# Selective-scan kernel: one quad of states from dt*u scaled by ScalarE and turned by TensorE, other units for the diagonals, both halves' softplus in one place

## The chip, the cores and the metric

One Trainium2 chip, one NeuronCore. The metric is the device time of one execution of the whole program in microseconds (us), lower is better. The engines are TensorE (PE; its weight loads are listed as PEld), VectorE (DVE), ScalarE (ACT), GpSimd (POOL) and SyncE (SP), which issues most DMAs.

## What is computed

A block of a vision model on x of 8 x 64 x 64 x 96, float32: group norm, a two-dimensional selective scan (192 channels, 16 states, 4 directions over 4096 places), a residual, and a second layer with a spectral up- and downsampling. The change lies in the scan alone:

```python
xs = ...                                   # (8, 4 directions, 192, 4096)
x_dbl = einsum('bkdl,kcd->bkcl', xs, x_proj_w)
dts, Bs, Cs = x_dbl[:, :, :6], x_dbl[:, :, 6:22], x_dbl[:, :, 22:]
delta = softplus(einsum('bkrl,kdr->bkdl', dts, dt_proj_w) + dt_proj_b)
A = -exp(A_logs)
def step(h, inp):                          # over the 4096 places
    ul, dl, Bl, Cl = inp
    h = exp(dl[..., None] * A) * h + (dl * ul)[..., None] * Bl[:, :, None, :]
    return h, einsum('bkdn,bkn->bkd', h, Cl)
y = ys + xs * Dk
```

## The kernel before

The program has three phases, one after the other: the first makes the scan's input xa and the gate, the second (`scan_phase`, from L309) does the scan, the third sums the directions and does everything behind. The change is in the second.

**Chunks, steps, units.** The scan is cut into 128 chunks: 8 images x 4 directions x 4 pieces of TC = 1024 places, in the order of `KORDER`. A chunk has two steps, one for each half of 96 channels; `un` counts units, 12 in a step (numbers 0 to 11 are the even step, 12 to 23 the odd one). A unit is 128 rows (4 states x 32 channels) x 1024 places: the 16 states are four groups g of four ("quads"), the 96 channels three thirds j = x % 3. `ORDER` = (2, 2, 2, 0, 3, 3, 3, 0, 1, 1, 1, 0) names the group of each of the 12 units.

**One unit**: ACT makes the decay E = exp(A * delta) (L841) from `dlr`, delta repeated by DMA. PE writes the drive dt*u*B into a PSUM bank ("fill"). DVE scans (L761) into H. POOL multiplies H by C (L961, "weigh") into HC. PE sums HC over the states (L700, `sum_y`, six matmuls for each half of the columns of three units).

**Three sorts of fill.** Group 0 is DIRECT: PE spreads B by `selb` (L642) and DVE multiplies it by `dur`, dt*u repeated by DMA (L742). The other three are DIAGONAL: PE multiplies the turned dt*u (`dluT`, weights of 32 columns) by diagonal matrices that hold B, 32 matmuls for a unit (L677; each float32 matmul is two records). The diagonals of groups 3 and 1 are made by ACT (L831, 64 multiplications of 128 x 128 in a chunk, `DIAGS` says how many after which unit), those of group 2 by POOL (L950, two in a chunk, after the weighing of units 17 and 19: `POOL_AT` = (6, 8) in the odd step).

**Side jobs in the row of PE.** `x` projects u for the next chunk (L627), `dt` makes the input of softplus (L636), `lt` turns dt*u of a step (L657; before an even step also B, L652). ACT copies the projection (L795, L796), DVE splits it (L736), ACT does softplus (L807) with a table load before it and another before the next exp, POOL makes dt*u (L942), ACT copies the turned block (L820). Units and side jobs take the three PSUM banks (`NP`) of `ring` in turn: each must wait until what stood in its bank three places earlier is released (a unit by its scan, `x` by DVE's split, `dt` by softplus, `lt` by ACT's copy).

**Other waits that order the work.** H has 4 buffers, so DVE scans unit un only after POOL weighed un - 4. E has 3. HC has 6, so POOL weighs un only after the sum over the group that ended at un - 4 or before (`y_summed`). The sum for the first group of a step also adds, in a second direction, what an earlier direction stored (L690), and for direction 0 a skip term (L696). `dlr` has 5 slots (`NSLOT`), `dur` 3 (`NDUR`); SP issues their loads in the order that `sync` writes out, and waits in it. The lines that set the row of side jobs:

```python
            if x == 1:
                jobs += [("lt", n + 1)]
            if x == 4 and c < NCHUNK:
                jobs += [("x", c)]
```

## Time and profile before

| | us |
|---|---|
| median of 3 runs (lowest, highest) | 11437.5 (11436.28, 11439.11) |
| the profiled execution: time, span | 11433.25, 11431.5 |
| PE busy, matmuls | 10219.9 (89%) |
| DVE busy | 9414.9 (82%) |
| ACT busy | 8518.6 (75%) |
| POOL busy | 9042.7 (79%) |
| mean granted clock of TensorE | 0.960 |

The span is from the first to the last instruction; the execution's own time is 1.75 us more. The first scan starts at 648.84 us and the scan phase ends near 9800 us, so it takes four fifths of the time. Matmuls are pipelined and their ends are modelled, so a busy PE isn't PE at its peak. A row of the waits says which engine and line waited, whose instruction ended the wait, how long in total, how often and the longest.

### The profile page before, as it was taken

Reading aid. Unit: us, or ns where it says so; the run is one execution under the profiler, and the core shown is the slowest. Engines: PE = TensorE matmul, PEld = TensorE weight load, DVE = VectorE, ACT = ScalarE, POOL = GpSimd, SP = SyncE. Lnnn points to the kernel's source line nnn. Section 1 sums busy time; section 2 is a strip of 40 time slices with the busy share of each in tenths; the row PEclk is TensorE's granted clock in tenths of the full one; section 3 lists DMA queues with packets and bytes.
Section 4 is the critical chain, followed back from the end, with each engine's and each line's share of the span. In section 5 each row is a group of like instructions: output and inputs, shape, how many; then the busy total and the mean of one; then the engine's idle time right before and its main releaser. Section 6 shows DMA issues by size and latency. Waiting matters only on the chain. (4 is left out here: it accounts for less than half of the span.)

```text
span 11431.5 us, 430806 instructions
## 1 busy us (share of the span) xinstructions
PE 10219.9 (89%) x185900; PEld 7314.0 (64%) x185900; DVE 9414.9 (82%) x5727; ACT 8518.6 (75%) x15618; POOL 9042.7 (79%) x3978
## 2 busy tenths in 40 slices
PE   8988898889988888899889888998898889799999
PEld 5656666666666666666666666666666666488888
DVE  7868888888888888888888888888888888555554
ACT  3478888888888888888888888888888888355454
POOL 1169999998999999999999999899999999634340
PEclk9989999999999999999999999999999999899999
DMA  3355666566656665666566656665666566322220
...
DMA packets 547581, 1653.42 MB, mean 145 GB/s; under 512 B 148562, under 2 KB 149362, under 8 KB 542872
## 3 DMA queue, kind: packets, MB, share of 16 engines
...
## 5 line engine op out<-in xcount | busy, mean ns | idle before, releaser
L961 POOL TENSOR_TENSOR HC<-H,crep 128x1024 f32<-128x1024 f32 x3072 | 7210.9, 2380 | 720.7 <-PE psum L700 681.7
L761 DVE TENSOR_TENSOR_SCAN H<-E,car,psum 128x1024 f32<-128x1024 f32 x2304 | 5282.4, 2334 | 535.7 <-PE psum L677 282.8
L841 ACT ACTIVATE E<-dlr,am 128x1024 f32<-128x1024 f32 x3072 | 3468.7, 1144 | 1335.2 <-DVE H L761 1311.3
L677 PE MATMUL psum<-diag,dluT 128*32 128x128 f32 x98304 | 3225.5, 275 | 360.1 <-DVE H L761 354.4
L677 PEld LDWEIGHTS psum<-diag,dluT 128*32 128x32 f32 x98304 | 2761.2, 110 | 1094.4 <-DVE H L761 702.8
L831 ACT ACTIVATE diag<-idn,blt 128x128 f32<-128x128 f32 x8192 | 2512.4, 389 | 42.5 <-PE psum L677 41.8
L677 PE MATMUL psum<-diagp,dluT 128*32 128x128 f32 x49152 | 1812.7, 302 | 656.8 <-POOL diagp L950 537.0
L677 PEld LDWEIGHTS psum<-diagp,dluT 128*32 128x32 f32 x49152 | 1636.5, 123 | 1027.7 <-issue 826.8
L700 PE MATMUL psum<-HC,sely 128*32 128x512 f32 x12288 | 2152.4, 598 | 22.5 <-POOL HC L961 21.3
L761 DVE TENSOR_TENSOR_SCAN H<-E,psum 128x1024 f32<-128x1024 f32 x768 | 1718.1, 2276 | 227.8 <-PE psum L677 84.9
L742 DVE TENSOR_TENSOR psum<-dur,psum 128x1024 f32<-128x1024 f32 x768 | 929.9, 1211 | 5.1 <-PE psum L642 1.1
L700 PEld LDWEIGHTS psum<-HC,sely 128*32 128x32 f32 x12288 | 431.4, 110 | 409.9 <-issue 365.6
L642 PE MATMUL psum<-sx,selb 96*128 96x512 f32 x1536 | 587.8, 463 | 7.1 <-DVE H L761 7.0
L642 PEld LDWEIGHTS psum<-sx,selb 96*128 96x128 f32 x1536 | 249.7, 189 | 431.8 <-DVE H L761 230.8
L1643 POOL TENSOR_TENSOR y<-y,tmp 96x1024 f32<-96x1024 f32 x60 | 189.6, 3210 | 417.0 <-DMA tmp<-scr_yk 417.0
L950 POOL TENSOR_SCALAR_AFFINE_SELECT diagp<-blt 128x2048 f32<-128x2048 f32 x256 | 514.9, 2012 | 2.0 <-ACT blt L816 2.0
L627 PE MATMUL psum<-u,wx 96*128 96x512 f32 x1024 | 475.7, 607 | 20.2 <-DVE dtw L773 20.2
L942 POOL TENSOR_TENSOR dlu<-dlt,u 96x1024 f32<-96x1024 f32 x128 | 340.0, 2656 | 175.4 <-ACT dlt L807 175.4
L1358 PEld LDWEIGHTS psum<-w2s,hs 128*100 128x100 f32 x4800 | 447.3, 168 | 15.2
L736 DVE TENSOR_TENSOR sx<-psum,sx 38x1024 fp32r<-38x1024 f32 x128 | 157.1, 1228 | 357.4 <-ACT sx L796 357.4
L1358 PE MATMUL psum<-w2s,hs 128*100 128x96 f32 x4800 | 447.8, 252 | 0.0
L45 PE MATMUL psum<-xp,wtap 96*96 96x512 f32 x1728 | 417.0, 400 | 0.0
(140 smaller groups left out, 9403.0 us busy)
## 6 DMA issues: line engine op xcount, KB each, us to landing
...
crep<-scr_bc SPq DMA_DIRECT2D x512, 256.0 KB, 4.9
crep<-scr_bc SPq DMA_DIRECT2D x1024, 128.0 KB, 3.0
scr_dlu<-dlu SPq DMA_DIRECT2D x256, 384.0 KB, 3.1
scr_yk<-yt ACTq DMA_DIRECT2D x256, 384.0 KB, 3.1
scr_dl<-dlt ACTq DMA_DIRECT2D x128, 384.0 KB, 4.0
scr_dl<-yt ACTq DMA_DIRECT2D x128, 384.0 KB, 4.6
```

The costliest lines, as they stand in the source:

```text
L45: r = e.matmul(o, w[p], x[q], start=first and i == 0, stop=last and i == 2)
L627: r = e.matmul(o, wx[:, k, h, :], x, start=h == 0, stop=h == 1)
L642: r = e.matmul(o[:, sub * 512:(sub + 1) * 512], selb[:], sx[0:C, c % 2, sub * 512:(sub + 1) * 512], start=True, stop=True)
L677: r = e.matmul(bank("unit", un)[32 * q:32 * q + 32, i * 128:(i + 1) * 128], dluT[:, m % 2, i, 32 * j:32 * j + 32], diagp[:, q, i, :] if g ...
L700: r = e.matmul(yps[32 * j:32 * j + 32, cols], sely[:], HC[:, (3 * i + j) % NHC, cols], start=g == 0 and k != 0 and not second(m), stop=g = ...
L742: e.tensor_tensor(bank("unit", un), dur[:, dur_slot(m, j), :], bank("unit", un), ALU.mult).then_inc(mul_done)
L761: e.tensor_tensor_scan(H[:, un % NH, ::step], decay[:, ::step], drive[:, ::step], init, ALU.mult, ALU.add).then_inc(scan_done)
L831: e.mul(diag[:, blk, 4 * a + q, :], idn[:], blt[:, n:n + 1]).then_inc(diag_made)
L841: e.activation(E[:, un % NE, :], dlr[:, slot(m, j), :], ACT.Exp, scale=am[:, ae:ae + 1]).then_inc(exp_done)
L950: e.affine_select(diagp[:, part * n:(part + 1) * n, :, :].rearrange("p q k t -> p (q k) t"), blt[:, lo:lo + n * NBLK].unsqueeze(2).to_broa ...
L961: e.tensor_tensor(HC[:, un % NHC, :], H[:, un % NH, :], crep[:, g, :], ALU.mult).then_inc(hc_done)
L1358: r = e.matmul(o[0:NU, i * C:(i + 1) * C], hs[:, q % 2, j, i * NU:(i + 1) * NU], w2s[:, j, :], start=j == 0, stop=j == 2)
```

## The change

Group 2 gets its diagonals from ACT and group 3 from POOL (before: 3 and 1 from ACT, 2 from POOL). Group 1 has no diagonals any more: ACT multiplies `dluT` of both halves by B (`sdl`, 32 multiplications of 128 x 192 in a chunk), and PE fills each unit by 8 transposes of 128 x 128. `DIAGS` now counts both sorts of multiplication, over units 14 to 28. The turning of B becomes a side job of its own, `bt`, at unit 10; both `lt` jobs stand in the odd step, at units 13 and 18, and none in the even one. The second `dt` stands at unit 7 (before 8), and ACT does both softplus one after the other at unit 8. POOL makes its diagonals one unit later. `dlr` has 4 slots, `dur` 2, and SP's order is another. A part of the diff that only renames or declares is left out.

```diff
@@ -310,21 +310,20 @@
-    GDIAG, GPOOL, GDIRECT = (3, 1), 2, 0
+    GDIAG, GPOOL, GSCALE, GDIRECT = 2, 3, 1, 0
-    DIRECT, DIAGONAL = 0, 1
+    DIRECT, DIAGONAL, SCALED = 0, 1, 2
     ORDER = (2, 2, 2, 0, 3, 3, 3, 0, 1, 1, 1, 0)
-    KIND = tuple(DIRECT if g == GDIRECT else DIAGONAL for g in ORDER)
-    ON = GDIAG + (GPOOL,)
+    KIND = tuple(DIRECT if g == GDIRECT else SCALED if g == GSCALE else DIAGONAL for g in ORDER)
+    ON = (GDIAG, GSCALE, GPOOL)
-    DIAGS = (0, 0, 3, 8, 4, 3, 7, 17, 0, 0, 0, 11, 9, 2, 0, 0, 0, 0, 0, 0, 0, 0, 0, 0)
-    DIAG_AT = 15
+    DIAGS = (3, 5, 3, 3, 5, 5, 3, 5, 4, 5, 5, 5, 5, 4, 4, 0, 0, 0, 0, 0, 0, 0, 0, 0)
-    POOL_AT = (6, 8)
-    NSLOT = 5
-    NDUR = 3
+    POOL_AT = (7, 9)
+    NSLOT = 4
+    NDUR = 2
...
@@ -352,9 +351,10 @@
-    diag = T("diag", [128, NBLK, 4 * len(GDIAG), 128])
+    diag = T("diag", [128, 4, NBLK, 128])
+    sdl = T("sdl", [128, NBLK, 2, NJ, 4, 32])
     diagp = T("diagp", [128, 4, NBLK, 128])
-    dluT = T("dluT", [128, 2, NBLK, C])
+    dluT = T("dluT", [128, NBLK, 2, C])
@@ -373,7 +373,7 @@
-    NACT = 4 * NBLK * len(GDIAG)
+    NACT = 4 * NBLK
...
@@ -486,25 +488,28 @@
         c = n // 2 + 1
         jobs = []
         if n % 2 == 0:
-            if x == 1:
-                jobs += [("lt", n + 1)]
             if x == 4 and c < NCHUNK:
                 jobs += [("x", c)]
             if x == 6 and c < NCHUNK:
                 jobs += [("dt", 2 * c)]
-            if x == 8 and c < NCHUNK:
+            if x == 7 and c < NCHUNK:
                 jobs += [("dt", 2 * c + 1)]
-        elif x == 1 and c < NCHUNK:
-            jobs += [("lt", 2 * c)]
+            if x == 10 and c < NCHUNK:
+                jobs += [("bt", c)]
+        elif c < NCHUNK:
+            if x == 1:
+                jobs += [("lt", 2 * c)]
+            if x == 6:
+                jobs += [("lt", 2 * c + 1)]
         return jobs
 
-    ring = [("x", 0), ("dt", 0), ("lt", 0), ("dt", 1)] + [("unit", un) for un in range(FILL_AHEAD)]
+    ring = [("x", 0), ("dt", 0), ("bt", 0), ("lt", 0), ("dt", 1), ("lt", 1)] + [("unit", un) for un in range(FILL_AHEAD)]
     for un in range(NUNIT):
         if un + FILL_AHEAD < NUNIT:
             ring += [("unit", un + FILL_AHEAD)]
         ring += side_jobs(*divmod(un, 12))
     place_of = {job: i for i, job in enumerate(ring)}
-    released = {"unit": scan_done, "x": sx_split, "dt": dl_made, "lt": lt_copied}
+    released = {"unit": scan_done, "x": sx_split, "dt": dl_made, "bt": bt_copied, "lt": lt_copied}
 
     def bank(*job):
@@ -537,8 +542,9 @@
 
         def in_dur(m, j):
             e.wait_ge(dlu_out, 16 * (m + 1))
-            if m:
-                e.wait_ge(mul_done, muls(last_of(m - 1, j=j, kinds=(DIRECT,))) + 1)
+            if NJ * m + j >= NDUR:
+                mb, jb = divmod(NJ * m + j - NDUR, NJ)
+                e.wait_ge(mul_done, muls(last_of(mb, j=jb, kinds=(DIRECT,))) + 1)
             i = dur_slot(m, j)
             for q in range(4):
@@ -579,20 +585,19 @@
             in_crep(0, i)
         out_dlu(0)
         for j in range(NJ):
-            in_dur(0, j)
             in_dlr(0, j)
+            if j < NDUR:
+                in_dur(0, j)
         out_dlu(1)
         for n in range(NSTEP):
             c = n // 2 + 1
             more = n + 1 < NSTEP
             if more:
                 in_dlr(n + 1, 0)
-                in_dlr(n + 1, 1)
             if n % 2 == 0 and n:
                 in_crep(c - 1, 1)
                 in_crep(c - 1, 2)
-            if more:
-                in_dur(n + 1, 0)
+            in_dur(n, 2)
             if n % 2 and n + 2 < NSTEP:
                 out_dlu(n + 2)
             load_y(n + 1)
@@ -600,14 +605,15 @@
                 next_rows(n - 2, 1)
                 next_rows(n - 2, 0)
             if more:
+                in_dur(n + 1, 0)
+                in_dlr(n + 1, 1)
                 in_dlr(n + 1, 2)
-                in_dur(n + 1, 1)
             if n % 2 and c < NCHUNK:
                 in_crep(c, 0)
             if n % 2 == 0 and n + 2 < NSTEP:
                 out_dlu(n + 2)
             if more:
-                in_dur(n + 1, 2)
+                in_dur(n + 1, 1)
@@ -643,14 +649,17 @@
+        def turn_b(c):
+            o = bank("bt", c)
+            bank_free(e, "bt", c)
+            e.wait_ge(sx_split, c + 1)
+            for k in range(NBLK):
+                r = e.matmul(o[:, NDIAG * k:NDIAG * (k + 1)], sx[0:C, c % 2, k * 128:(k + 1) * 128], selt[:], start=True, stop=True)
+            r.then_inc(bt_done)
+
         def turn(m):
             o = bank("lt", m)
             bank_free(e, "lt", m)
-            if m % 2 == 0:
-                e.wait_ge(sx_split, m // 2 + 1)
-                for k in range(NBLK):
-                    e.matmul(o[:, BLT_AT + NDIAG * k:BLT_AT + NDIAG * (k + 1)], sx[0:C, m // 2 % 2, k * 128:(k + 1) * 128],
-                             selt[:], start=True, stop=True)
             e.wait_ge(dlu_made, m + 1)
             for k in range(NBLK):
                 at = k // 4 * 512 + k % 4 * C
@@ -665,17 +674,22 @@
             if kind(un) == DIRECT:
                 e.wait_ge(sx_split, m // 2 + 1)
                 spread(bank("unit", un), m // 2).then_inc(fill_done)
+            elif kind(un) == SCALED:
+                e.wait_ge(scaled, NACT * (m // 2 + 1))
+                for i in range(NBLK):
+                    r = e.transpose(bank("unit", un)[:, i * 128:(i + 1) * 128],
+                                    sdl[:, i, m % 2, j, :, :].rearrange("p q d -> p (q d)"), idn[:])
+                r.then_inc(fill_done)
             else:
...
@@ -806,29 +824,50 @@
 
+        def turn_b(c):
+            e.wait_ge(bt_done, c + 1)
+            if c:
+                e.wait_ge(diag_made, NACT * c)
+                e.wait_ge(scaled, NACT * c)
+                e.wait_ge(pool_diag_made, PARTS * c)
+            e.copy(blt[:].rearrange("p (n k) -> p k n", k=NBLK),
+                   bank("bt", c)[:, 0:NBLK * NDIAG].rearrange("p (k n) -> p k n", n=NDIAG)).then_inc(bt_copied)
+
         def turn(m):
             o = bank("lt", m)
             e.wait_ge(lt_done, m + 1)
-            if m % 2 == 0:
-                if m:
-                    e.wait_ge(diag_made, NACT * (m // 2))
-                    e.wait_ge(pool_diag_made, PARTS * (m // 2))
-                e.copy(blt[:].rearrange("p (n k) -> p k n", k=NBLK),
-                       o[:, BLT_AT:BLT_AT + NBLK * NDIAG].rearrange("p (k n) -> p k n", n=NDIAG)).then_inc(bt_copied)
             if m >= 2:
                 e.wait_ge(fill_done, last_of(m - 2, kinds=(DIAGONAL,)) + 1)
-            e.copy(dluT[:, m % 2, :, :].rearrange("p (s k) c -> p s (k c)", s=2),
-                   o.rearrange("p (s x) -> p s x", s=2)[:, :, 0:NBLK // 2 * C]).then_inc(lt_copied)
-
-        def diagonal(c, first, n):
+                e.wait_ge(scaled, NACT * (m // 2))
+            e.copy(dluT[:, :, m % 2, :].rearrange("p (s k) c -> p s k c", s=2),
+                   o.rearrange("p (s x) -> p s x", s=2)[:, :, 0:NBLK // 2 * C].rearrange("p s (k c) -> p s k c", c=C)).then_inc(lt_copied)
+
+        def diagonal(c, i):
+            if i == 0:
+                e.wait_ge(bt_copied, c + 1)
+                if c:
+                    e.wait_ge(fill_done, last_of(2 * c - 1, g=GDIAG) + 1)
+            q, blk = divmod(i, NBLK)
+            n = 4 * NBLK * ON.index(GDIAG) + i
+            e.mul(diag[:, q, blk, :], idn[:], blt[:, n:n + 1]).then_inc(diag_made)
+
+        def scale(c, i):
+            if i == 0:
+                e.wait_ge(bt_copied, c + 1)
+                e.wait_ge(lt_copied, 2 * c + 2)
+                if c:
+                    e.wait_ge(fill_done, last_of(2 * c - 1, g=GSCALE) + 1)
+            q, blk = divmod(i, NBLK)
+            n = 4 * NBLK * ON.index(GSCALE) + i
+            e.mul(sdl[:, blk, :, :, q, :].rearrange("p h j d -> p (h j) d"),
+                  dluT[:, blk, :, :].rearrange("p h (j d) -> p (h j) d", d=32), blt[:, n:n + 1]).then_inc(scaled)
+
+        def weights(c, first, n):
             for i in range(first, first + n):
-                a, blk, q = i // (4 * NBLK), i // 4 % NBLK, i % 4
-                if i == 0:
-                    e.wait_ge(bt_copied, c + 1)
-                if c and i % (4 * NBLK) == 0:
-                    e.wait_ge(fill_done, last_of(2 * c - 1, g=GDIAG[a], kinds=(DIAGONAL,)) + 1)
-                n = NBLK * (4 * a + q) + blk
-                e.mul(diag[:, blk, 4 * a + q, :], idn[:], blt[:, n:n + 1]).then_inc(diag_made)
+                if i < NACT:
+                    diagonal(c, i)
+                else:
+                    scale(c, i - NACT)
 
         def exp(un):
             if un >= NUNIT:
@@ -886,15 +925,17 @@
         delta(0)
         out_dl(0)
+        turn_b(0)
         turn(0)
         delta(1)
         out_dl(1)
+        turn(1)
         e.wait_ge(a_made, 2)
         made = sum(DIAGS[:24 - DIAG_AT])
-        diagonal(0, 0, min(made, 4 * NBLK))
+        weights(0, 0, NACT)
         exp(0)
         exp(1)
-        diagonal(0, min(made, 4 * NBLK), max(0, made - 4 * NBLK))
+        weights(0, NACT, made - NACT)
         for un in range(NUNIT + 12):
             n, x = divmod(un, 12)
             c = n // 2 + 1
@@ -915,21 +956,22 @@
             if n == NSTEP:
                 continue
             if n % 2 == 0:
-                if x == 2:
-                    turn(n + 1)
                 if x == 5 and c < NCHUNK:
                     project(c)
                 if x == 8 and c < NCHUNK:
                     delta(2 * c)
-                if x == 10 and c < NCHUNK:
                     delta(2 * c + 1)
+                if x == 11 and c < NCHUNK:
+                    turn_b(c)
             elif c < NCHUNK:
                 if x == 4:
                     turn(2 * c)
+                if x == 8:
+                    turn(2 * c + 1)
             y = (12 * n + x - DIAG_AT) % 24
             d = c if 12 * (n % 2) + x >= DIAG_AT else c - 1
             if d < NCHUNK:
-                diagonal(d, sum(DIAGS[:y]), DIAGS[y])
+                weights(d, sum(DIAGS[:y]), DIAGS[y])
 
     def pool(e):
         def delta(m):
@@ -961,9 +1003,9 @@
             e.tensor_tensor(HC[:, un % NHC, :], H[:, un % NH, :], crep[:, g, :], ALU.mult).then_inc(hc_done)
 
         delta(0)
+        delta(1)
         for part in range(PARTS):
             diagonal(0, part)
-        delta(1)
         for un in range(NUNIT + 1):
             n, x = divmod(un, 12)
```

How the written order moves the instructions, at three places of a chunk in the middle of the program.

ACT, from unit 7 on of an even step: L807 (now L825) is softplus, L841 (L880) exp, L848 (L887) the copy of the carries. Before:

```order
L848 COPY car<-H 128x2
L807 ACT_TABLE_LOAD
L807 ACTIVATE dlt<-psum,dtb 96x1024
L841 ACT_TABLE_LOAD
L841 ACTIVATE E<-dlr,am 128x1024
L864 DMA scr_dl<-dlt 96x1024
L841 ACTIVATE E<-dlr,am 128x1024
L848 COPY car<-H 128x2
L807 ACT_TABLE_LOAD
L807 ACTIVATE yt<-psum,dtb 96x1024
L841 ACT_TABLE_LOAD
L841 ACTIVATE E<-dlr,am 128x1024
```

Now:

```order
L887 COPY car<-H 128x2
L825 ACT_TABLE_LOAD
L825 ACTIVATE dlt<-psum,dtb 96x1024
L825 ACTIVATE yt<-psum,dtb 96x1024
L880 ACT_TABLE_LOAD
L880 ACTIVATE E<-dlr,am 128x1024
L903 DMA scr_dl<-dlt 96x1024
L880 ACTIVATE E<-dlr,am 128x1024
L903 DMA scr_dl<-yt 96x1024
L887 COPY car<-H 128x2
L880 ACTIVATE E<-dlr,am 128x1024
```

Both softplus stand behind one table load, and two table loads of four are gone; the copy of B (L833) has come in at unit 11.

PE, from the fill of unit 3 of an even step on (in a first direction other than 0): L642 (now L648) fills a direct unit, L677 (L691) a diagonal one, L657 (L666) turns dt*u, L627 (L633) projects, L700 (L714) sums. Before:

```order
L642 MATMUL psum<-sx,selb 128x512 x2
L657 MATMUL psum<-idn,dlu 128x96 x8
L677 MATMUL psum<-diag,dluT 32x128 x32
L700 MATMUL psum<-HC,sely 32x512 x3
L677 MATMUL psum<-diag,dluT 32x128 x32
L700 MATMUL psum<-HC,sely 32x512 x3
L677 MATMUL psum<-diag,dluT 32x128 x32
L627 MATMUL psum<-u,wx 128x64x8 x4
L642 MATMUL psum<-sx,selb 128x512 x2
L700 MATMUL psum<-HC,sely 32x512 x3
L677 MATMUL psum<-diag,dluT 32x128 x32
L700 MATMUL psum<-HC,sely 32x512 x3
```

Now:

```order
L648 MATMUL psum<-sx,selb 128x512 x2
L691 MATMUL psum<-diagp,dluT 32x128 x32
L714 MATMUL psum<-HC,sely 32x512 x3
L691 MATMUL psum<-diagp,dluT 32x128 x32
L714 MATMUL psum<-HC,sely 32x512 x3
L691 MATMUL psum<-diagp,dluT 32x128 x32
L633 MATMUL psum<-u,wx 128x64x8 x4
L648 MATMUL psum<-sx,selb 128x512 x2
L714 MATMUL psum<-HC,sely 32x512 x3
L680 MATMUL psum<-idn,sdl 128x128 x8
L714 MATMUL psum<-HC,sely 32x512 x3
L642 MATMUL psum<-sx,dtw 96x512 x2
```

The turning is gone from between the fills of units 3 and 4, and the fill of unit 8 is eight transposes (L680) where it was 32 matmuls.

SP, one even step and the beginning of the odd one: dlr is delta repeated, dur is dt*u repeated, crep C repeated, four DMAs for a third. Before:

```order
L553 DMA dlr<-scr_dl 32x1024 x8
L562 DMA crep<-scr_bc 32x1024 x8
L544 DMA dur<-scr_dlu 32x1024 x4
L553 DMA dlr<-scr_dl 32x1024 x4
L544 DMA dur<-scr_dlu 32x1024 x4
L536 DMA scr_dlu<-dlu 96x1024
L544 DMA dur<-scr_dlu 32x1024 x4
L553 DMA dlr<-scr_dl 32x1024 x8
L544 DMA dur<-scr_dlu 32x1024 x4
L536 DMA scr_dlu<-dlu 96x1024
L523 DMA u<-scr_xa 96x1024 x2
```

Now:

```order
L559 DMA dlr<-scr_dl 32x1024 x4
L568 DMA crep<-scr_bc 32x1024 x8
L550 DMA dur<-scr_dlu 32x1024 x8
L559 DMA dlr<-scr_dl 32x1024 x8
L541 DMA scr_dlu<-dlu 96x1024
L550 DMA dur<-scr_dlu 32x1024 x4
L559 DMA dlr<-scr_dl 32x1024 x4
L550 DMA dur<-scr_dlu 32x1024 x4
L541 DMA scr_dlu<-dlu 96x1024
L528 DMA u<-scr_xa 96x1024 x2
L550 DMA dur<-scr_dlu 32x1024 x4
```

Before, two thirds of dlr were issued first; now one, then a third of dur for the current step and one for the next, and behind these the other two of dlr, in the four slots.

## Rows read from the trace of the kernel before

**Rows 1.** Window: us; busy of PE, PEld, DVE, ACT, POOL; clock, DMA share, GB/s

```profile
7000.00:8000.00 1000.00, 896.67 (x18272) 614.78 (x18268) 879.72 (x435) 821.46 (x1546) 913.01 (x393) 0.97 0.62 162
```

**Rows 2.** Waits from 3000 to 8000 us: who for whom, total us, times, longest

```profile
POOL HC L961 <- PE psum L700: 368.4, 183, 6.4
PE psum L677 <- POOL diagp L950: 298.5, 71, 5.3
...
POOL dlu L942 <- ACT dlt L807: 36.6, 27, 1.4
```

**Rows 3.** Groups by line, 3000 to 8000 us: busy us, mean ns | idle before, releasers

```profile
L961 POOL TENSOR_TENSOR HC<-H,crep 128x1024 f32<-128x1024 f32 x1683 | 3951.0, 2381 | 382.3 <-PE psum L700 368.4 <-DVE H L761 13.4
```

**Rows 4.** Timeline of POOL: start, us, instructions, idle before them in brackets

```profile
4589.63 7.03 POOL L961 TENSOR_TENSOR HC<-H,crep 128x1024 f32<-128x1024 f32 x3 [0.89 <-PE psum L700]
4599.07 2.35 POOL L961 TENSOR_TENSOR HC<-H,crep 128x1024 f32<-128x1024 f32 x1 [2.41 <-PE psum L700]
...
4744.42 4.72 POOL L961 TENSOR_TENSOR HC<-H,crep 128x1024 f32<-128x1024 f32 x2 [4.42 <-PE psum L700]
...
5032.35 4.71 POOL L961 TENSOR_TENSOR HC<-H,crep 128x1024 f32<-128x1024 f32 x2 [6.17 <-PE psum L700]
```

**Rows 5.** Timeline of a chunk, 5000 to 5032 us, start and us first

```profile
5002.14 3.70 PE L677 MATMUL psum<-diagp,dluT 128*32 128x128 f32 x128 [2.60 <-POOL diagp L950]
...
5011.58 0.82 PE L657 MATMUL psum<-idn,dlu 96*128 96x96 f32 x8
5012.53 1.21 DVE L742 TENSOR_TENSOR psum<-dur,psum 128x1024 f32<-128x1024 f32 x1
5012.68 1.95 PE L677 MATMUL psum<-diag,dluT 128*32 128x128 f32 x64 [0.28 <-DVE H L761]
5013.13 3.32 ACT L831 ACTIVATE diag<-idn,blt 128x128 f32<-128x128 f32 x11
5013.78 6.82 DVE L761 TENSOR_TENSOR_SCAN H<-E,car,psum 128x1024 f32<-128x1024 f32 x3
...
5020.66 3.70 PE L627 MATMUL psum<-u,wx 96*128 96x512 f32 x8
5025.52 1.02 PE L696 MATMUL psum<-u,dg 96*96 96x512 f32 x2
5026.48 1.23 DVE L736 TENSOR_TENSOR sx<-psum,sx 38x1024 fp32r<-38x1024 f32 x1 [2.65 <-ACT sx L796]
5031.10 1.06 PE L700 MATMUL psum<-HC,sely 128*32 128x512 f32 x6
```

**Rows 6.** Windows of 6 us around two low stretches of PE, columns as in rows 1

```profile
3564.00:3570.00 6.00, 3.01 (x32) 0.88 (x21) 4.78 (x4) 5.94 (x16) 6.00 (x4) 1.00 0.85 204
3570.00:3576.00 6.00, 4.16 (x80) 4.19 (x84) 3.79 (x3) 5.78 (x16) 6.00 (x3) 0.50 1.02 219
3384.00:3390.00 6.00, 3.37 (x96) 2.64 (x98) 5.96 (x4) 3.15 (x5) 4.72 (x2) 1.00 0.75 194
```

**Rows 7.** More groups by line, 3000 to 8000 us, columns as in rows 3

```profile
L841 ACT ACTIVATE E<-dlr,am 128x1024 f32<-128x1024 f32 x1681 | 1898.2, 1144 | 720.7 <-DVE H L761 709.9 <-issue 0.2
L831 ACT ACTIVATE diag<-idn,blt 128x128 f32<-128x128 f32 x4499 | 1380.0, 389 | 22.9 <-PE psum L677 22.9
L642 PE MATMUL psum<-sx,selb 96*128 96x512 f32 x842 | 321.9, 463 | 0.0
L807 ACT ACT_TABLE_LOAD x140 | 179.6, 1283 | 2.6
L807 ACT ACTIVATE dlt<-psum,dtb 96x1024 f32<-96x1024 f32 x70 | 77.8, 1112 | 0.8
```

**Rows 8.** Loads of dlr: one third's issue on SP, and all landings from 3000 us on

```profile
5030.79 1.76 SPq L553 DMA_DIRECT2D dlr<-scr_dl  x4
DMA to landing us min/median/max: 2.1/4.0/10.2
```

**Rows 9.** Window across the start of a chunk, columns as in rows 1

```profile
5066.00:5090.00 24.00, 20.39 (x492) 14.90 (x487) 21.87 (x12) 22.09 (x58) 24.00 (x11) 1.00 1.03 241
```

More of the change, by code:

```diff
@@ L390, in scan_phase @@
     lt_copied = sem("lt_copied")
+    bt_done = sem("bt_done")
     bt_copied = sem("bt_copied")
     diag_made = sem("diag_made")
+    scaled = sem("scaled")
     dl_out = [sem(f"dl_out{i}") for i in range(2)]
@@ L438, in last_of @@
                    if want.get("g", place(un)[5]) == place(un)[5] and want.get("j", un % 3) == un % 3
-                   and kind(un) in want.get("kinds", (DIRECT, DIAGONAL)))
+                   and kind(un) in want.get("kinds", (DIRECT, DIAGONAL, SCALED)))
     def slot(m, j):
@@ L673, in fill @@
                 else:
[L674 removed]
+                    e.wait_ge(diag_made, NACT * (m // 2 + 1))
                 for i in range(NBLK):
@@ L713, in side_job @@
                 delta(n)
+            elif name == "bt":
+                turn_b(n)
             else:
@@ L718, in tensor @@
         side_job("dt", 0)
+        side_job("bt", 0)
         side_job("lt", 0)
         side_job("dt", 1)
+        side_job("lt", 1)
         for un in range(FILL_AHEAD):
@@ L906, in scalar @@
                     out_dl(2 * c)
-                if x == 11:
+                if x == 10:
                     out_dl(2 * c + 1)
@@ L1732, in constants @@
     for i in range(12):
-        src = (12, 4, 8)[i // 4] + i % 4
+        src = (8, 4, 12)[i // 4] + i % 4
         selt[src, i] = 1
```

6 lines of the change are left out of this document (2 added, 4 removed).

## Prediction

> **What bounds it now.** The sum is made against the profiled execution, 11433.25 us, which is 4.3 below the median; the medians given are the sum plus 4. I read the windows first, to see whether the scan phase is even. It is: in a window of 1000 us POOL is busy for 91% [rows 1], PE for 90% as matmuls are modelled, DVE 88%, ACT 82%, so four engines are near the bound and what matters is who lets whom idle. The number of exps [rows 7] gives the pace: 1681 / 24 = 70.0 chunks in 5000 us, **71.4 us a chunk**, 128 chunks.
>
> Then the waits [rows 2]. POOL idles for 368.4 us on PE's sums, 36.6 on softplus and 13.4 on DVE [rows 3]: 418 us, **5.98 a chunk**; the other 65.4 it works without a gap. PE waits for POOL's diagonals once a chunk, 298.5 / 70 = 4.3 us. That is the most visible stall, but POOL is busy all through it, so it costs only what it makes late behind it. The timeline of POOL [rows 4] tells where its idle time lies, always in the even step: 0.6 to 0.9 us ahead of weighing unit 0 and of unit 3, then ahead of unit 6, where it waits for the sum of the step's first group. This last one is 2.4 us in a first direction other than 0, 4.4 with one extra term in the sum (second direction, or direction 0), 6.2 with both.
>
> The timeline of that place [rows 5] shows the chain: the turning (5011.58) takes a bank and holds the next fills back by one scan; the projection of 3.70 us starts at 5020.66, after them; then come spread, first half of the sum, fill of unit 8, second half, ending at 5032.16, 0.2 before POOL goes on. DVE's split waits 2.65 us in the same place, for ACT's copies of the projection.
>
> **The change, part by part.**
>
> *POOL's diagonals go to group 3.* They are needed by the fill of unit 4 of the next step, not unit 0, that is some four units of 2.3 us or more later, while POOL makes them one unit later. PE's wait of 4.3 us ends. What it hides today is only in POOL's own shadow; the gain is what follows: the sums ahead of units 0 and 3 are no more late (1.5 us a chunk). What is late next: group 2, made by ACT now, whose 32 multiplications are done at unit 21 while PE fills unit 24 at its place 22; PE could wait some 0.3 us there, hidden by the two filled banks.
>
> *No turning in the even step.* The fills of units 4 and 5 wait for a scan one earlier, and the projection for the scan of unit 4. The turning in the odd step takes a bank at unit 18; there the units behind it are the cheap transposed ones, and POOL has its diagonals to do, so I cost it at nothing; with the cover gone it is 0.82 us of PE [rows 5] a chunk, 105 us in all.
>
> *Transposed fill.* Eight transposes of 96 columns took 0.82 us [rows 5]; with 128 columns on both sides I scale by 256/224 to 0.94, call it 1.0, against 1.95 for a diagonal unit [rows 5]. Six units a chunk: 5.7 us of PE. Bounds: 0.82 below, and 1.95 above if nothing is won. PE is not the bound once its stalls are gone, so only the fill of unit 8 pays, since it stands between the two halves of the sum POOL waits for: 1 us.
>
> *ACT.* Two table loads of 1283 ns go [rows 7], -2.57 us a chunk. The 32 multiplications of 192 columns replace 32 of 128: from 128 to 1024 columns a duration grows from 389 to 1144 ns, 0.84 ns a column, so 64 columns are 54 ns and 32 times that 1.7 us. Bounds: nothing, and in proportion to size, half of the 307 ns between starts (1380.0 us over 4499), 4.9 us. ACT goes from 58.7 to about 58 us a chunk. Not on the path, unless bunched: in the seven units from 22 to 28 it has 7 x 1.14 + 32 x 0.36 + carries = 20.2 us, against some 18 of DVE; its lead of two units (4.6 - 1.1 = 3.5 us) covers that.
>
> *Both softplus together.* Two of three banks are held from PE's place 6 and 7 to ACT's place 8. Unit 10 must then wait for the first softplus. I cost this inside the next step.
>
> *Fewer slots.* dur with two and dlr with four give loads less lead. I cost them at nothing: two thirds (1.76 us of issue each) and a median landing of 4.0 us [rows 8] are 7.5 us behind the multiplication of unit 7; the exp of unit 13 can't start before the scan of unit 10 ends, 9.1 us after it (three scans took 6.82 us [rows 5]). Cover gone: the slower rival below.
>
> **The new chain, step by step.** Time 0 is POOL's end of weighing unit 20 (four before unit 0 of the next step), when DVE may scan unit 0. POOL: a diagonal of 2.0, then nine weighings of 2.35 (3951.0 / 1683 [rows 3]): unit 5 is done at **23.1**. DVE, held by H's four buffers, ends unit 1 at 6.7, 2 at 9.0, 3 at 12.5 (1.21 for the multiplication), 4 at 14.8, 5 at 17.1, 6 at 19.4. PE: fill of unit 6 12.5 to 14.5, projection 14.8 to 18.5, spread 19.3 (two records of 0.38 [rows 7]), half sum 20.3, fill of unit 8 at 21.3, half sum at **22.4**; 24.4 with one extra term (2 x 1.02), 26.5 with two. So POOL idles 0, 1.3 or 3.4 us ahead of unit 6. ACT's copies (2.1, from the projection's end to the split's start [rows 5]) end at 20.6, DVE's split at 21.8, the multiplication at 23.0, unit 7 at 25.3, no later than POOL has done unit 6. Then exp, table load and softplus 1.14 + 1.28 + 1.11 [rows 7] end at 28.8; POOL reaches its dt*u at 27.8 in the plain chunk: 1.0 more. With the 48, 64 and 16 chunks of the three sorts: (48 x 1.0 + 64 x 1.3 + 16 x 3.4) / 128 = 1.45. For handovers this leaves out I take 0.3, **1.75 us of idle time a chunk**. The filling of unit 10 is ready at about 29.7, when DVE has just scanned units 8 and 9.
>
> Gain: (5.98 - 1.75) x 128 = 541 us. The prologue now turns both halves and makes 32 diagonals ahead of the first exp: +5. The sum is 11433 + 5 - 541 = 10897, so I forecast **10900**; its own range is 10800 to 11020, from idle times of 1.0 and 2.7.
>
> **The rivals.**
>
> *Partial* (0.13). The projection doesn't come earlier, because ACT's bunch or another bank holds it; only the 1.5 us ahead of units 0 and 3 go. For it: ACT is busy for 82% [rows 1]. Against: its bunch begins five units earlier now. 128 x 1.5 = 192 us: 11240.
>
> *The clock* (0.12). The granted clock fell to 0.50, 1.2 GHz of 2.4, for a window of 6 us; in the window before it PE had worked 3.01 us of 6 and then waited for POOL's diagonals [rows 6]. With the wait gone this drop goes. But units 8 to 10 now give PE only 1.0 + 0.7 of 2.7 us each, 63% and in pieces. The nearest row, 3.37 in 6 (56%) at full clock [rows 6], speaks against a drop. If both steps had one, 6 us at half clock leave 3 us of work undone, of which the slack of PE takes half: 2 x 1.5 x 128 = 384 us back, 11280. The Trainium skill, "TensorE: Matmul & The Clock Gate", Part 4, says that transposes don't count as activity in the same way; by that rule the drop would come, and this rival holds. No row here has transposes long enough to show it.
>
> *Loads too late, slower* (0.08). SP waits at dur of the next step for the multiplication of unit 7, and both thirds of dlr stand behind it. At the start of a chunk the queues have a share of 1.03 for 24 us already [rows 9]. ACT may get dlr 9.1 + 3.5 = 12.6 us after that multiplication without DVE idling; the two issues take 3.5, so a landing of 9.1 is free and the longest today is 10.2 [rows 8], the median 4.0. It decides from 13.3 us of landing once a chunk, where 4.2 us a chunk are lost, the whole gain. At 16 it is 6.9 a chunk: (6.9 - 4.2) x 128 = 340 us slower than before, 11770.
>
> *Nothing changes* (0.03). The multiplications cost their upper bound and ACT, at 61 us a chunk and bunched, comes to hold POOL: about 11430.
>
> *More than forecast* (0.04). POOL's idle time all but ends, 0.6 a chunk: 10745.
>
> **How the numbers follow.** Forecast 0.60, and the others as given. The likeliest gives 10900. The range runs from 10780 to 11290: it takes in the forecast's own range, the partial gain and the clock, and leaves out the late loads, no change and most of the better case, some 0.15. A measurement of this kernel can tell about 0.2%, 23 us, from no change. Faster: 0.60 + 0.13 + 0.12 + 0.04, less a little for what adds up: 0.88. Same 0.03, slower 0.09.
>
> **What would show it.** Right: POOL busy for some 97% of a window of 1000 us; a chunk of 67 us (24 exps); no wait of PE on POOL's diagonals; no idle time of POOL ahead of units 0 and 3, and 0, 1 to 2 and 3 to 4 us ahead of unit 6 by sort; eight transposes in 0.9 to 1.1 us; 140 table loads in a stretch that had 280; a mean clock near 1. Wrong: a wait of ACT on the DMA of dlr (late loads), windows with a clock of 0.5 after units 8 to 10 (clock), waits of DVE on ACT's exps (multiplications dearer than 0.4 us), or POOL idling at new places, above all behind the paired softplus at unit 10.

## The result and the profile after

| | before | changed |
|---|---|---|
| median of 4 runs, us | 11438.31 (11436.28 to 11441.46) | 11190.65 (11184.67 to 11195.45) |
| ratio, 95% interval | | 0.9786 (0.9775 to 0.9798) |
| span of the profiled execution, us | 11431.5 | 11183.0 |
| mean granted clock | 0.960 | 0.943 |

The change makes the kernel faster by 248 us, 2.1%. The forecast was 10900, a gain of 537: right in direction, the time inside the range, but more than twice too large. The window and the waits of GpSimd in the changed kernel, the answers to [rows 1] and [rows 2], columns as there:

```profile
7000.00:8000.00 1000.00, 880.62 (x14025) 551.42 (x14026) 904.25 (x448) 826.59 (x1551) 939.12 (x404) 0.95 0.64 166
```

```profile
POOL HC L1003 <- PE psum L714: 188.1, 171, 3.8
POOL dlu L984 <- ACT dlt L825: 64.8, 64, 1.4
POOL HC L1003 <- DVE H L779: 40.7, 31, 5.3
```

No wait of PE on GpSimd's diagonals is left. The number of exps from 3000 to 8000 us is 1728 (1681 before), so a chunk takes 69.4 us (71.4). GpSimd idles 4.1 us of it, where it idled 6.0 and was to idle 1.75. Its busy time per chunk is the same within 0.1 us, 65.3. Adding up the idle times of GpSimd by the unit ahead of which it idles, over 24 weighings a chunk, gives the table on which the rest of this text rests (us a chunk, 3000 to 8000 us, small places left out):

| ahead of unit | before | forecast | changed |
|---|---|---|---|
| 0 and 3 | 1.44 | 0 | 0.16 |
| 6 | 3.84 | 1.07 | 1.22 |
| 7 | 0.17 | 0 | 0.15 |
| dt*u at 8 (waits for softplus) | 0.52 | 0.38 | 0.90 |
| 9 | 0 | 0 | 0.64 |
| 12 | 0 | 0 | 1.00 |
| left for handovers | | 0.30 | |
| all | 5.97 | 1.75 | 4.10 |

What the prediction worked out at units 0, 3 and 6 came out to within 0.2 us on average. By sort of chunk the idle time ahead of unit 6 is 0, 1.5 and 4.2 us, where 0, 1.3 and 3.4 were forecast. What it missed stands at units 8 to 12: 2.54 us instead of 0.38. The timeline of the changed kernel there, in a plain chunk (start, us, idle time in brackets; L680 is a transposed fill, L642 softplus's input, L825 softplus, L714 a sum):

```profile
4419.56 6.82 DVE L779 TENSOR_TENSOR_SCAN H<-E,car,psum 128x1024 f32<-128x1024 f32 x3
4421.96 1.09 PE L680 MATMUL psum<-idn,sdl 128*128 128x128 f32 x8 [2.88 <-DVE H L779]
4424.19 1.17 PE L642 MATMUL psum<-sx,dtw 102*96 102x512 f32 x2 [1.14 <-DVE H L779]
4424.55 1.11 ACT L825 ACTIVATE dlt<-psum,dtb 96x1024 f32<-96x1024 f32 x1
4425.56 1.10 ACT L825 ACTIVATE yt<-psum,dtb 96x1024 f32<-96x1024 f32 x1
4425.71 1.97 PE L680 MATMUL psum<-idn,sdl 128*128 128x128 f32 x8 [0.34 <-ACT dlt L825]
4425.73 2.87 POOL L984 TENSOR_TENSOR dlu<-dlt,u 96x1024 f32<-96x1024 f32 x1 [1.40 <-ACT dlt L825]
4427.61 1.93 PE L714 MATMUL psum<-HC,sely 128*32 128x512 f32 x6
4427.72 2.35 DVE L779 TENSOR_TENSOR_SCAN H<-E,car,psum 128x1024 f32<-128x1024 f32 x1 [1.34 <-PE psum L680]
4431.71 2.35 POOL L1003 TENSOR_TENSOR HC<-H,crep 128x1024 f32<-128x1024 f32 x1 [0.76 <-PE psum L714]
```

PE waits 2.88 us for the scan of unit 7, then for that of unit 8, then for softplus, because the units from 7 on and the two inputs of softplus share three banks: the fill of unit 9 takes the bank of unit 7, the second input that of unit 8, and the fill of unit 10 that of the first input. The eight transposes of unit 9 still take 1.09 us, those of unit 10 take 1.97, and the half sum behind them 1.93 where [rows 5] had 1.06: the clock has dropped in between. VectorE idles 1.34 us for the fill of unit 10, GpSimd afterwards 0.76. From 3000 to 8000 us the transposes of unit 10 take more than 1.6 us in 57 of 72 chunks, 1.81 on average, and VectorE idles 1.19 us a chunk ahead of its scan; those of unit 8, ahead of all the pauses, always take 1.09. Windows of 3 us in another chunk show the same drop (columns as in rows 1):

```profile
5123.00:5126.00 3.00, 1.83 (x13) 1.10 (x10) 3.00 (x2) 0.92 (x1) 2.56 (x2) 1.00 0.70 198
5126.00:5129.00 3.00, 1.51 (x5) 0.60 (x4) 3.00 (x2) 2.97 (x5) 2.28 (x2) 0.59 1.04 240
5129.00:5132.00 3.00, 3.00 (x14) 1.56 (x13) 1.54 (x2) 2.97 (x3) 3.00 (x2) 0.50 1.00 287
```

Two groups of ACT for the terms of its sum (columns as in rows 3):

```profile
L862 ACT ACTIVATE sdl<-dluT,blt 128x192 f32<-128x192 f32 x2304 | 847.8, 443 | 0.0
L825 ACT ACT_TABLE_LOAD x72 | 92.4, 1283 | 1.3
```

A multiplication of 192 columns lasts 443 ns against 389 for 128: 54 ns more, as worked out. Table loads are halved.

### The profile page after: what moved, and what is told of

It is laid out like the page before. It is cut to its first block and busy times, and to the rows that moved or that the text cites. A ratio compares the mean times of both kernels' runs of the same rounds, so it can differ in the third digit from the quotient of the medians.

```text
span 11183.0 us, 345048 instructions
## 1 busy us (share of the span) xinstructions
PE 9904.4 (89%) x142892; PEld 6561.4 (59%) x142892; DVE 9415.5 (84%) x5727; ACT 8368.0 (75%) x15364; POOL 9038.0 (81%) x3978
## 5 line engine op out<-in xcount | busy, mean ns | idle before, releaser
L880 ACT ACTIVATE E<-dlr,am 128x1024 f32<-128x1024 f32 x3072 | 3498.4, 1145 | 994.4 <-DVE H L779 944.9
L714 PE MATMUL psum<-HC,sely 128*32 128x512 f32 x12288 | 2343.4, 644 | 89.2 <-POOL HC L1003 62.4
L691 PE MATMUL psum<-diagp,dluT 128*32 128x128 f32 x49152 | 1636.6, 277 | 249.1 <-DVE H L779 236.2
L691 PE MATMUL psum<-diag,dluT 128*32 128x128 f32 x49152 | 1694.1, 276 | 130.5 <-issue 110.7
L691 PEld LDWEIGHTS psum<-diagp,dluT 128*32 128x32 f32 x49152 | 1391.5, 111 | 672.2 <-DVE H L779 486.4
L691 PEld LDWEIGHTS psum<-diag,dluT 128*32 128x32 f32 x49152 | 1428.0, 111 | 467.0 <-issue 401.1
L862 ACT ACTIVATE sdl<-dluT,blt 128x192 f32<-128x192 f32 x4096 | 1507.2, 443 | 0.0
L680 PE MATMUL psum<-idn,sdl 128*128 128x128 f32 x6144 | 1001.2, 316 | 512.6 <-DVE H L779 441.0
L680 PEld LDWEIGHTS psum<-idn,sdl 128*128 128x128 f32 x6144 | 791.9, 160 | 906.3 <-DVE H L779 589.1
L852 ACT ACTIVATE diag<-idn,blt 128x128 f32<-128x128 f32 x4096 | 1304.3, 392 | 0.0
L714 PEld LDWEIGHTS psum<-HC,sely 128*32 128x32 f32 x12288 | 407.1, 113 | 623.7 <-issue 465.0
L648 PE MATMUL psum<-sx,selb 96*128 96x512 f32 x1536 | 641.4, 501 | 1.6 <-issue 1.3
L648 PEld LDWEIGHTS psum<-sx,selb 96*128 96x128 f32 x1536 | 259.5, 205 | 649.3 <-issue 607.6
L633 PE MATMUL psum<-u,wx 96*128 96x512 f32 x1024 | 475.5, 607 | 41.4 <-DVE dtw L791 21.2
```

What stands on the lines that cost most here:

```text
L648: r = e.matmul(o[:, sub * 512:(sub + 1) * 512], selb[:], sx[0:C, c % 2, sub * 512:(sub + 1) * 512], start=True, stop=True)
L680: r = e.transpose(bank("unit", un)[:, i * 128:(i + 1) * 128], sdl[:, i, m % 2, j, :, :].rearrange("p q d -> p (q d)"), idn[:])
L691: r = e.matmul(bank("unit", un)[32 * q:32 * q + 32, i * 128:(i + 1) * 128], dluT[:, i, m % 2, 32 * j:32 * j + 32], diagp[:, q, i, :] if g ...
L714: r = e.matmul(yps[32 * j:32 * j + 32, cols], sely[:], HC[:, (3 * i + j) % NHC, cols], start=g == 0 and k != 0 and not second(m), stop=g = ...
L852: e.mul(diag[:, q, blk, :], idn[:], blt[:, n:n + 1]).then_inc(diag_made)
L862: e.mul(sdl[:, blk, :, :, q, :].rearrange("p h j d -> p (h j) d"), dluT[:, blk, :, :].rearrange("p h (j d) -> p (h j) d", d=32), blt[:, n: ...
```

## The experiments

Three theories were to be told apart: that the missing gain lies in the bank places of the side jobs (paired softplus, B turned apart at unit 10), that it lies in the low clock, and that it lies in the transposed fill itself or in the parts undone one by one. All ratios are to runs of the kernel before on the same chip; 0.001 is 11.4 us. The changed kernel was not timed side by side with these runs, so ratios (its own is 0.9786) are compared.

**e1, softplus apart.** In the changed kernel (the store of the second half goes from 10 to 11 with it):

```diff
-            if x == 7 and c < NCHUNK:
+            if x == 8 and c < NCHUNK:
                 jobs += [("dt", 2 * c + 1)]
...
                 if x == 8 and c < NCHUNK:
                     delta(2 * c)
+                if x == 10 and c < NCHUNK:
                     delta(2 * c + 1)
```

> The changed kernel with one part undone: the second half's softplus stands again two units behind the first (its TensorE job at unit 8, ScalarE at unit 10). Theory, the pair holds two of three PSUM banks until ScalarE's place at unit 8, so that the fill of unit 10 waits for it, VectorE idles 1.3 us and GpSimd afterwards 0.8 us ahead of unit 9 and 1.0 us ahead of unit 12: with it apart these idle times go, 1.8 x 128 = 230 us less than the changed kernel's 11191, about 10960, though ScalarE gets its two table loads back. Rival, the idle time there comes from the low clock that the transposes bring, not from the banks: within 40 us of 11191.

11104.48 us, ratio 0.9715 (0.9701 to 0.9730): 81 us less than the changed kernel. The idle time ahead of unit 9 fell from 0.64 to 0.05; that ahead of unit 12 fell only from 1.00 to 0.91. VectorE's waits for the transposed fills from 3000 to 8000 us, in the changed kernel and in e1:

```profile
DVE H L779 <- PE psum L680: 90.0, 80, 1.5
DVE H L779 <- PE psum L680: 4.6, 8, 0.7
```

So the pair costs, and it costs ahead of unit 9; unit 12 is another cause. The rival, in which the banks cost next to nothing, falls. But the clock moved too (mean 0.955 instead of 0.943, the fill of unit 10 1.54 us on average instead of 1.81), so the 81 us are those of the pair with the part of the clock that hangs on it.

**e2, softplus early.** e1, and `delta(2 * c)` of ScalarE at `x == 7`, its store at 8.

> As the kernel with softplus apart, and ScalarE does the first half's softplus one unit earlier, at unit 7, ahead of the exp that waits for the scan of unit 7. Theory, GpSimd waits 1.4 us for softplus before its dt*u in most plain chunks (64.8 us in 72 chunks, 0.9 a chunk) and this wait goes: 100 us less than the kernel with softplus apart. Rival, GpSimd only waits later, for the scan of unit 8 or a sum: no more than 30 us less.

11044.63, ratio 0.9662 (0.9647 to 0.9676): 61 us less than e1. The wait for softplus (0.90) is gone, but 0.57 came up ahead of unit 9: GpSimd, now earlier, overtakes a sum. 61 of the theory's 100 us.

**e3, the swap alone.** In the kernel before (the rows of `selt` follow the groups):

```diff
-    GDIAG, GPOOL, GDIRECT = (3, 1), 2, 0
+    GDIAG, GPOOL, GDIRECT = (2, 1), 3, 0
-    DIAGS = (0, 0, 3, 8, 4, 3, 7, 17, 0, 0, 0, 11, 9, 2, 0, 0, 0, 0, 0, 0, 0, 0, 0, 0)
+    DIAGS = (0, 5, 5, 6, 5, 5, 6, 5, 5, 0, 0, 8, 8, 6, 0, 0, 0, 0, 0, 0, 0, 0, 0, 0)
-    POOL_AT = (6, 8)
+    POOL_AT = (7, 9)
```

> The kernel before with one part of the change alone: GpSimd makes the diagonals of group 3 (needed at unit 4) and ScalarE those of groups 2 and 1. Theory, TensorE's wait of 4.3 us a chunk for GpSimd's diagonals goes and with it the idle time of GpSimd ahead of units 0 and 3, 1.5 us a chunk: 190 us less than before, about 11250, and a mean clock near 1.0 in the scan. Rival, ScalarE's 32 diagonals of group 2 come too late for the fill of unit 0 of the next chunk, and a wait for ScalarE takes the place of the one for GpSimd: within 50 us of before.

11355.75, ratio 0.9938 (0.9922 to 0.9955): 71 us less than before, not 190. PE's wait for the diagonals, 4.3 us a chunk and the profile's most visible stall, is gone, and GpSimd's idle time fell from 5.97 to 5.18: 1.44 to 0.59 ahead of units 0 and 3, 3.84 to 3.73 ahead of unit 6. The mean clock of the whole span went from 0.960 only to 0.968.

**e4, turned twice.** In the changed kernel the loop of `fill` over the blocks of a scaled unit runs twice:

```diff
-                for i in range(NBLK):
+                for i in list(range(NBLK)) * 2:
```

> The changed kernel with each of the eight transposes of a scaled unit done twice into the same place (the output is the same): about 1.0 us more of TensorE for each of six units of a chunk. Theory, TensorE is on the path only where the fill of unit 8 stands between the halves of a sum and at units 9 and 10: 1 to 2 us a chunk, 130 to 260 us more than the changed kernel's 11191. If transposes keep the clock up as matmuls do, the windows at 0.5 after unit 8 go and some of it comes back. Rival, TensorE has slack there, so the time stays within 40 us.

11210.22, ratio 0.9809 (0.9794 to 0.9824): 26 us more, and the intervals overlap, so it can't be told from the changed kernel. The rival's 40 us hold. Ahead of unit 6 the idle time rose from 1.22 to 2.04, as the theory had it, and ahead of unit 12 from 1.00 to 1.22, but ahead of unit 9 it fell from 0.64 to 0.01 and ahead of dt*u from 0.90 to 0.53: GpSimd idles as much as before, 4.16 us a chunk, at other places. The 16 transposes of a fill mostly take 1.97 us, 0.98 for eight (up to 3.63 in 17 of 72 chunks at unit 9). At unit 10 the doubled fill at full clock is thus as long as the single one at half clock, and VectorE idles 0.99 us a chunk for it, against 1.19. The window from 3000 to 8000 us of e4, and the same of the changed kernel behind it:

```profile
3000.00:8000.00 5000.00, 4534.83 (x72856) 3056.23 (x72854) 4512.24 (x2230) 4144.78 (x7767) 4699.34 (x2014) 0.98 0.65 166
```

```profile
3000.00:8000.00 5000.00, 4376.31 (x69539) 2747.92 (x69536) 4519.66 (x2233) 4132.64 (x7776) 4703.66 (x2016) 0.94 0.64 166
```

More transposes, a higher clock: here they kept it up, and PE is busy for 63.1 us a chunk instead of 60.8, though some 6 us of transposes at full clock were put in. The rule of the Trainium skill that the prediction weighed ("TensorE: Matmul & The Clock Gate", Part 4), that transposes don't count as activity in the same way, isn't borne out by this run.

**e5, the pair alone.** The edit of e1 turned round, in the kernel before (second input at unit 7, both softplus at 8, the second store at 10).

> The kernel before with the pairing of the softplus alone (second TensorE job at unit 7, both softplus at unit 8, two table loads of four gone). Theory, the fill of unit 10 then waits for the first softplus and GpSimd waits ahead of units 9 or 12; but here GpSimd has idled 3.8 us ahead of unit 6 and lags the sums less, so the pair costs less than the 80 us it cost in the changed kernel: 0 to 80 us more than before. Rival, fewer table loads help ScalarE and the time falls by more than 20 us.

11433.28, ratio 1.0001 (0.9992 to 1.0011): nothing, in either direction. VectorE's waits for the diagonal fills, in the kernel before and in e5:

```profile
DVE H L761 <- PE psum L677: 200.5, 192, 4.6
DVE H L761 <- PE psum L677: 287.3, 323, 5.3
```

The difference stands ahead of unit 10: 0.02 us a chunk before, 1.17 in e5, as much as in the changed kernel (1.19). So the pair makes VectorE wait here too, and it reaches nobody: GpSimd's idle time is 0 ahead of unit 9 and 3.82 ahead of unit 6, as before. The same step that costs 81 us in the changed kernel is free where GpSimd has just idled 3.8 us ahead of unit 6 and isn't early for the sums behind. The two table loads that go with it, 2.57 us of ACT a chunk, bring nothing that shows.

**e6, the bank held again.** In the changed kernel:

```diff
+            if x == 1:
+                jobs += [("hold", n // 2)]
...
+        def hold(c):
+            o = bank("hold", c)
+            bank_free(e, "hold", c)
+            for k in range(NBLK):
+                at = k // 4 * 512 + k % 4 * C
+                r = e.transpose(o[:, at:at + C], idn[0:C, :], idn[0:C, 0:C])
+            r.then_inc(hold_done)
```

and at unit 2 of the even step ScalarE copies 600 columns of it into a tile that nothing reads.

> The changed kernel with a job put back where the turning stood in the even step: at unit 1 TensorE turns eight constant blocks into a bank of the ring, and ScalarE copies 600 columns of it at unit 2 (the results go nowhere). Theory, the turning's place was the larger part of GpSimd's wait ahead of unit 6: it comes back by 1.5 us a chunk, 190 us more than the changed kernel, about 11380. Rival, the wait shrank by the cheaper fill of unit 8 and by the clock, and the place was worth little: less than 60 us.

11481.36, ratio 1.0044 (1.0029 to 1.0059): 295 us more than the changed kernel, and slower than before. GpSimd's idle time rose by 2.3 us a chunk, from 4.10 to 6.39; its waits (compare the three rows of the changed kernel above):

```profile
POOL HC L1023 <- PE psum L727: 320.0, 242, 4.9
POOL HC L1023 <- DVE H L794: 64.4, 34, 5.3
POOL dlu L1004 <- ACT dlt L840: 61.1, 61, 1.4
```

Ahead of unit 6 it is 3.01 (1.22), ahead of unit 3 0.37 (0.03), ahead of unit 7 0.40 (0.15). Theory right in kind, and the place costs half as much again as expected: 0.8 us of PE, 0.7 of ACT and one place in the ring cost more than the whole change brings.

**e7 and e8, B turned later.** e2, and `("bt", c)` at unit 12 with ScalarE's copy at 13 (e7), or at 11 and 12 (e8):

```diff
-            if x == 10 and c < NCHUNK:
-                jobs += [("bt", c)]
         elif c < NCHUNK:
+            if x == 0:
+                jobs += [("bt", c)]
```

> The kernel with the early softplus apart (11045), and the turning of B goes from unit 10 to unit 12, ScalarE's copy of it from 11 to 13. Theory, the bank it takes is what makes the fill of unit 14 and with it the sum ahead of unit 12 late (GpSimd idles 0.86 us a chunk there); behind unit 12 the late sum is the one ahead of unit 15, where GpSimd has its dt*u to make: 0.9 x 128 = 110 us less, about 10935. Rival, two side jobs at units 12 and 13 hold two banks, and the idle time moves to units 15 to 18: within 30 us.

> As the kernel with B turned at unit 12, but at unit 11 (ScalarE's copy at 12). Theory, the fill of unit 14 still waits for the scan of unit 12 if the bank is taken ahead of it: no, at unit 11 the job stands behind the fill of unit 13, the fill of 14 waits for the scan of unit 12 and the first half of the sum comes before: half the gain, 50 us less than 11045. Rival, as much as at unit 12, 110 us.

e7: 11007.83, ratio 0.9629 (0.9614 to 0.9643), 38 us less than e2. e8: 11017.51, ratio 0.9641 (0.9625 to 0.9657), 24 us less. In e7 the idle time ahead of unit 12 fell from 0.89 to 0, so the bank of `bt` was its cause; 0.27 came up ahead of unit 15 and 0.10 more ahead of unit 6, and of the 110 us expected 38 are left. In e8 it is 0.71. The interval of e7 lies below that of e2; that of e8 overlaps both, so it can be told from neither.

**e9, kept busy.** The changed kernel, and in `delta` of TensorE, for even m, the two matmuls four times over:

```diff
-            for sub in range(2):
+            for sub in list(range(2)) * (4 if m % 2 == 0 else 1):
```

> The changed kernel with the two matmuls that make the first half's softplus input done four times over into the same place (the output is the same): 2.1 us more of TensorE in the gap of 2.9 us in which it waits for the scan of unit 7. Theory, the low clock behind unit 8 comes from this gap and doubles the fill of unit 10 (1.97 us against 1.09) and the sums (1.93 against 1.03); kept busy, the clock stays and part of the idle time ahead of units 9 and 12 goes: 0.5 us a chunk, 60 us less than 11191, and the mean clock rises above 0.96. Rival, the banks alone set that idle time: within 25 us.

11127.5, ratio 0.9736 (0.9722 to 0.9751): **57 us faster for more work**. PE at the same units of the same chunk as above:

```profile
4399.11 2.08 PE L642 MATMUL psum<-sx,dtw 102*96 102x512 f32 x8
4402.66 1.09 PE L680 MATMUL psum<-idn,sdl 128*128 128x128 f32 x8 [1.48 <-DVE H L779]
4404.90 0.71 PE L642 MATMUL psum<-sx,dtw 102*96 102x512 f32 x2 [1.15 <-DVE H L779]
4406.42 1.34 PE L680 MATMUL psum<-idn,sdl 128*128 128x128 f32 x8 [0.81 <-ACT dlt L825]
4407.69 1.93 PE L714 MATMUL psum<-HC,sely 128*32 128x512 f32 x6
```

The gap is 1.48 us instead of 2.88, the clock falls later, and the fill of unit 10 takes 1.34 instead of 1.97 (on average 1.52 instead of 1.81). Idle time: 0.38 ahead of unit 9 (0.64), 0.81 ahead of unit 12 (1.00). So the low clock is a second cause beside the banks; the mean clock rose to 0.960, less than expected, and the half sum is still slow.

**e10 and e11, sums whole.** e7, and the first sum of a step made whole at unit 5 (e10), or every sum (e11):

```diff
-                sum_y((un - 5) // 3, (un - 5) % 3)
+                i, sub = divmod(un - 5, 3)
+                if i % NG:
+                    sum_y(i, sub)
+                elif sub == 0:
+                    sum_y(i, 0)
+                    sum_y(i, 1)
```

> The best kernel so far (B turned at unit 12, softplus apart and early: 11008), and the first sum of each step is made whole at unit 5, ahead of the fill of unit 8, where its second half stood behind it. Theory, GpSimd waits 1.0 us a chunk ahead of unit 6 for that second half, and the fill of 1.1 us between the halves is most of it: 0.8 x 128 = 100 us less, about 10910. Rival, the fill of unit 8 comes a microsecond or more later and VectorE waits for it: within 30 us.

> As the kernel with the first sum whole, for all sums. Theory, the other places (units 9, 12, 15, 0.8 us a chunk together) gain too: 150 us less than 11008. Rival, every third fill comes 1.0 us later, where a diagonal fill of 1.95 and a sum of 2.1 are more than a scan of 2.3, and VectorE waits: 50 us or more above the kernel with the first sum whole.

e10: 10985.43, ratio 0.9611 (0.9597 to 0.9626), 20 us less than e7 with intervals that overlap, so the rival's "within 30" holds: ahead of unit 6 the wait for PE fell only from 1.09 to 0.88, and those ahead of units 0, 9 and 15 rose. e11: 11074.39, ratio 0.9688 (0.9668 to 0.9707), 67 us more than e7 and 88 more than e10: its rival holds, the waits ahead of units 6 and 7 are 2.25 us.

**e12, both.** e10, and the matmuls of e9 three times over.

> The kernel with the first sum whole (10985), and the two matmuls for the first half's softplus done three times over, 1.4 us more of TensorE in its gap of 2.9 us; softplus starts at unit 7 here and gets its input 1.4 us later, just when its table is loaded. Theory, the low clock behind unit 8 costs here too (transposes of unit 10 1.97 us, the sum 1.93): 40 to 60 us less, about 10935, and a mean clock above 0.96. Rival, softplus and with it GpSimd's dt*u now come late, or the filler isn't enough to keep the clock: within 20 us of 10985 or above.

10970.45, ratio 0.9599 (0.9586 to 0.9612): 14 us below e10, not to be told from it. It is the lowest of all, faster than the changed kernel by 1.9% and than before by 4.0%.

## Why the prediction was right and wrong

**What bounds it: right.** GpSimd's busy time stayed at 65.3 us a chunk, and nearly the whole change of time is its idle time: 5.97 - 4.10 = 1.87 us x 128 = 239 of the 248 us.

**Diagonals by GpSimd for group 3: right in effect, mis-sized.** The wait of 4.3 us went, and it was right that it was hidden. But the 1.5 us ahead of units 0 and 3 were booked to it; e3 shows 0.85 from it alone. Most of the rest came with the turning's place: with a bank held at unit 1 again (e6) 0.37 stood ahead of unit 3, and e3 has 0.40 there.

**No turning in the even step: right, and the largest part.** The new chain put the end of the first sum at 22.4, 24.4 or 26.5 by sort, idle time 1.07 on average; measured 1.22. e6 prices the place at 295 us, more than the whole gain. The prediction gave it no price of its own.

**Transposed fill: right at full clock.** 1.09 us against 1.0 forecast, but 1.81 on average at unit 10, where the clock has dropped. That PE isn't the bound, e4 shows: with twice the work the time can't be told from the changed kernel's.

**ACT: right.** 54 ns a multiplication; table loads halved, and of no worth that shows (e5).

**Both softplus together, and B's turning: the step that failed.** "The filling of unit 10 is ready at about 29.7, when DVE has just scanned units 8 and 9", and beyond that the chain stopped: what lies behind unit 8 had the price of nothing. Two terms were missing. First, the fill of unit 10 came too late. Counted from the end of the scan of unit 7, the prediction had it ready 4.4 us later and the scan of unit 9 over at 4.6; in the plain chunk above they are 5.9 and 4.6, so VectorE idles 1.34 us. Of the 1.5 us too much, about 1.0 is the half clock of the eight transposes (1.97 us, costed at 1.0), the rest mostly the later softplus. With the pair apart 81 us come back (e1). Second, `bt` has no term at all; it stood ahead of the sum for unit 12, where 1.0 us a chunk was idle, and moving it gives 38 us net (e7). Both have one root: the chain was followed to unit 8 and GpSimd taken as lagging the sums from there on, as it did before. But it lagged then because it had idled at unit 6; with that gone it is early, and each late sum behind shows. e5 and e1 show it: the same pair makes VectorE wait 1.2 us in both kernels, and costs nothing before and 81 us after.

**Softplus ahead of dt*u: mis-sized.** 1.0 us in the plain chunks alone was forecast, 0.38 a chunk; it is 1.37 us in the plain ones and 0.73 in those with one extra term, 0.90 a chunk. Softplus one unit earlier is worth 61 us (e2).

**The clock: a rival that came, beside the forecast's own cause.** The drop is there, while GpSimd weighs unit 6 or 7, in 67 of 72 chunks, and 51 more stand in the odd step; in all PE runs at half clock for 645 us of the 5000, where it was 406. The ground that the prediction took from its rows fits: units 8 to 10 give PE little to do and in pieces, with pauses of 2.88 and 1.14 us for banks, and with more to do there the clock falls later (e9) or seldom (e4: 171 us at half clock). The other ground, that transposes don't count, isn't borne out (e4). The price of 384 us was not tested as a whole: e9 gets 57 back, from a part of it, and in e4 the clock's gain and the cost of the added work can't be told apart. Nor do the runs part clock and banks fully: the fill of unit 10 is late by both.

**Late loads, no change, partial gain: didn't come.** 11 waits of ACT on dlr, 23.2 us in 72 chunks, are 0.3 us a chunk; the longest landing is 12.9 us, the median 3.9.

Together e1, e2 and e7 give back 180 us of the 290 that were missing. e10 and e12 give 34 more. What is left, some 80 us, was followed to no single cause.

**PE's pauses without a named wait.** Near the start of 20 of the 72 chunks PE stands still for 1.8 to 4.9 us, 2.9 on average, and no semaphore explains it. Two windows of one such place (columns as in rows 1):

```profile
5168.00:5171.00 3.00, 0.00 (x0) 0.00 (x0) 2.76 (x2) 3.00 (x8) 3.00 (x3) 0.98 1.03 220
5171.00:5174.00 3.00, 2.68 (x28) 1.96 (x32) 1.25 (x1) 3.00 (x8) 3.00 (x2) 0.50 0.72 164
```

PE stands still while ACT, DVE and POOL work and the queues are full (1.03), and comes back at half clock. The packets of the DMA queues say more. A queue of its own (q8, of the kind "instruction") brings packets of 16384 bytes, one every 9 us. Each of the 21 pauses over 1.5 us without a named wait from 3000 to 8000 us ends 1.3 to 1.8 us after such a packet has landed; of the 78 pauses over 1.5 us with a named wait 2 do. In the kernel before it is 7 of 7. So PE most likely waits there for its own instructions, which come late behind the data; no run changed this. The pauses touch the forecast: by sort, chunks without one idle 0, 1.2 and 3.5 us ahead of unit 6, close to the 0, 1.3 and 3.4 worked out, and those with one 0.7 to 0.9 us more.

**Open.** The turning wasn't moved alone in the kernel before: its diagonals need `dluT` until unit 10, so it can't be without other edits; e6 is the reverse of it.
